# Splitting the search for each expert's first tokens over the end of one stage and the start of the next

## The reference

```python
xn = _layernorm(x, axis=-1)
s = _L0_attn_ref(xn, ...)      # two transformer blocks: norm, 2-head attention, norm, MLP of 512
g = _silu(_L0_ffn_ref(xn, ...))
x = x + s * g

# inside _L0_ffn_ref: 64 experts, each token goes to its 8 best, an expert keeps its first 64 tokens
probs = jax.nn.softmax(x @ router_w.T, axis=-1)
topk_w, topk_ids = jax.lax.top_k(probs, 8)
pos = jnp.cumsum(onehot, axis=0)[jnp.arange(N), flat_e] - 1
valid = pos < C                                   # C = 64
idx = jnp.where(valid, flat_e * C + pos, E * C)
x_buf = jnp.zeros((E * C + 1, x.shape[1]), x.dtype).at[idx].set(x[tok])
# per expert: silu(xb @ w_gate) * (xb @ w_up) @ w_down, weighted and added back to its tokens,
# plus a shared expert for all tokens
```

## Time and profile before

| | us |
|---|---|
| median of 3 runs | 1468.88 (1463.78 to 1471.66) |
| the profiled execution's own time | 1472.35 |
| its span in the trace | 1470.5 |
| TensorE matmuls busy | 1217.1 (83% of the span) |
| VectorE busy | 1017.4 (69%) |
| ScalarE busy | 784.7 (53%) |
| GpSimd busy | 655.8 (45%) |

### The profile page before, as it was taken

The page is one execution under the profiler, slowest core; times in us unless marked ns, Lnnn a source line. Parts: engine busy times, 40 slices in busy tenths (PEclk is TensorE's granted clock), DMA queues, the critical chain, the costliest instruction groups (busy, mean ns, idle before and its releaser), DMA issues. The chain is left out here.

```text
span 1470.5 us, 29231 instructions
## 1 busy us (share of the span) xinstructions
PE 1217.1 (83%) x7815; PEld 919.7 (63%) x7816; DVE 1017.4 (69%) x3639; ACT 784.7 (53%) x2010; POOL 655.8 (45%) x1270
## 2 busy tenths in 40 slices
PE   3999999999924999999999746568888888599993
PEld 2778777877722677777677534446666666366662
DVE  2777777777766777777777378757777777266663
ACT  1675656666512666566565356646666666233331
POOL 3343434434211545455454468714444444146665
PEclk9999999999966999999999855589999999699997
DMA  3433334242301221222212166534444444355562
GB/s 137 150 98 134 116 113 140 89 142 87 121 4 36 61 59 40 57 40 60 60 39 51 13 192 213 174 108 151 150 146 146 150 150 142 110 152 174 173 179 71
DMA packets 159257, 162.84 MB, mean 111 GB/s; under 512 B 20950, under 2 KB 138429, under 8 KB 159216
## 3 DMA queue, kind: packets, MB, share of 16 engines
q1 hardware_dynamic: 143936, 133.23, 29.0%
q0 software_dynamic: 14848, 26.77, 6.6%
q10 hardware_dynamic: 432, 2.38, 0.4%
HBM read 76.59 MB, written 71.04 MB: 100 GB/s over the span
## 5 line engine op out<-in xcount | busy, mean ns | idle before, releaser
L380 ACT ACTIVATE big<-ps,BHS 128x256 f32<-128x256 f32 x256 | 107.2, 470 | 61.1 <-PE ps L257 60.4
L257 PE MATMUL ps<-big,W 128*128 128x256 f32 x512 | 130.7, 400 | 5.9 <-ACT big L385 5.9
L392 ACT ACTIVATE pr<-ps,nmx 128x256 f32<-128x256 f32 x256 | 117.9, 473 | 27.4 <-DVE nmx L439 26.7
L270 PE MATMUL ps<-W,big 128*128 128x128 f32 x1024 | 130.9, 281 | 0.0
L270 PEld LDWEIGHTS ps<-W,big 128*128 128x128 f32 x1024 | 119.8, 192 | 13.9 <-ACT big L380 9.9
L2141 POOL DMA_INDIRECT out<-X,io x96 | 100.6, 1048 | 34.4 <-issue 34.4
L257 PEld LDWEIGHTS ps<-big,W 128*128 128x128 f32 x512 | 95.6, 197 | 27.3 <-ACT big L385 16.2
L1983 PE MATMUL ps<-big,zT 128*128 x192 | 103.3, 620 | 8.7 <-DVE pr L2079 8.4
L439 DVE TENSOR_REDUCE nmx<-ps 128x2 f32<-128x512 f32 x128 | 82.4, 686 | 40.4 <-PE ps L292 39.7
L1016 POOL DMA_INDIRECT ffn<-big,si x64 | 93.9, 1468 | 26.4 <-issue 26.4
L2057 ACT ACTIVATE pr<-ps 128x256 f32<-128x256 f32 x96 | 36.9, 384 | 108.2 <-PE ps L1983 108.2
(11 more groups left out here) (256 smaller groups left out, 3276.7 us busy)
## 6 DMA issues: line engine op xcount, KB each, us to landing
srt<-big SPq DMA_DIRECT2D x16, 1584.0 KB, 5.7
X<-srt SPq DMA_DIRECT2D x24, 800.0 KB, 4.6
big<-we SPq DMA_DIRECT2D x16, 768.0 KB, 4.9
rowd<-big SPq DMA_DIRECT2D x32, 272.0 KB, 2.2
big<-x SPq DMA_DIRECT2D x64, 128.0 KB, 2.2
X<-big SPq DMA_DIRECT2D x64, 128.0 KB, 2.1
big<-we SPq DMA_DIRECT2D x16, 384.0 KB, 3.5
X<-srt SPq DMA_DIRECT2D x24, 256.0 KB, 3.0
```

Source lines behind the costliest of these rows:

```text
L257: last = pe.matmul(pb[2 * g + f // 2][:, f % 2 * S:(f % 2 + 1) * S], W0[:, l, 512 + f * P:512 + (f + 1) * P], zT2[:, g, :], start=True, st ...
L270: last = pe.matmul(pb[4 + g][:, t * C:(t + 1) * C], hT[:, g, f, t * P:(t + 1) * P], W0[:, l, 1024 + f * C:1024 + (f + 1) * C], start=(f == ...
L380: act.activation(hT[:, g, f, :], pb[2 * g + half][:, f % 2 * S:(f % 2 + 1) * S], ACT.Silu, bias=BHS[:, l, f:f + 1], scale=GELU).then_inc(s ...
L392: last = act.activation(pr[:, g, h, t, :], pb[2 * g + h][:, t * S:(t + 1) * S], ACT.Exp, bias=nmx[:, g, h * TPU + t:h * TPU + t + 1], accu ...
```

## The change

The block `pick` is gone, with its two meetings of all engines reduced to the one between the stages. Its work is split:

- `bodies` takes a function `between`, called ahead of the last, feed-forward-only body. DVE in stage 1 passes one: it waits for all words (`keyT`, 16) and runs `pick_words`, the first search with its preparation and split (before: lines 909 to 906 of the first round). `result(0)` and `result(1)` come behind it.
- In stage 2 DVE does the statistics and the norm of pair 0 first and then `pick_tokens`: the second and third search, `firsts`, the wait for PE's turned list, and `gidx` and `sidx`. Only then comes the copy into `gi` that raises `idx`, and then the bodies.
- PE turns the list after its front for pair 0, then waits for a new semaphore `scaled`, and starts its bodies.
- POOL adds the unit matrix to W1 and scales W0 between its `front(0)` and its first `step`, and raises `scaled`.

The two functions and their helpers `largest` and `split` have the same instructions as before, on tiles of the same shapes.

```diff
-        def bodies(engine, step):
+        def bodies(engine, step, between=None):
             step(0, ffn=False)
             with engine.Fori(1, HALF - 1) as i:
                 step(i)
             step(HALF - 1, front=False)
+            if between:
+                between()
             step(HALF, att=False)
...
+        def pick_words(dve):
+            dve.scalar_tensor_tensor(work, words, 0.0, CST[0:E0, C_WORD:C_WORD + TOK // 16], ALU.is_gt, ALU.mult)
+            dve.drain()
+            dve.scalar_tensor_tensor(work, work, float(2 ** 24), words, ALU.subtract, ALU.add)
+            dve.drain()
+            largest(dve, work, -float(2 ** 25))
+            split(dve, 4, 3.0, 16, True)
+        def pick_tokens(dve):
+            largest(dve, work[:, 0:4 * CAP], 0.0)
+            split(dve, 1, 4.0, 1, False)
+            largest(dve, work[:, 0:4 * CAP], 0.0)
+            dve.tensor_copy(em[:, :], CST[0:CAP, C_ONE:C_ONE + E0]).then_inc(firsts, 1)
+            dve.wait_ge(turned_keys, 1)
...
+            dve.tensor_tensor(sidx[:, :], tk[:, :], em[:, :], ALU.add)
...
-                    bodies(dve, lambda i, att=True, ffn=True, front=True: body_vector(dve, s, i, 0, att, ffn, x))
+
+                    def between():
+                        dve.wait_ge(s["keyT"], HALF)
+                        pick_words(dve)
+                    bodies(dve, lambda i, att=True, ffn=True, front=True: body_vector(dve, s, i, 0, att, ffn, x), between)
         stage1()
...
-        pick()
...
                     front(0)
+                    for n in range(NP // C):
+                        pool.tensor_tensor(W1[:, n * C:(n + 1) * C], W1[:, n * C:(n + 1) * C], ident, ALU.add)
+                    pool.tensor_scalar(W0[:, 1, 1024:1536], W0[:, 1, 1024:1536], 1.0 / GELU, None, ALU.mult)\
+                        .then_inc(scaled, 1)
                     step(0, first=True)
...
                     x.front(pe, 0)
+                    pe.wait_ge(firsts, 1)
+                    for h in range(2):
+                        last = pe.matmul(pb[0][h * CAP:(h + 1) * CAP, 0:E0], lst[:, :], ident[0:E0, 0:E0],
+                                         start=True, stop=True)
+                    last.then_inc(turned_keys, 1)
+                    pe.wait_ge(scaled, 1)
                     bodies(pe, lambda i, att=True, ffn=True, front=True: body_tensor(pe, s, i, 1, att, ffn, x))
...
-                    dve.tensor_copy(gi[:, :], gidx[:, 0:EP]).then_inc(s["idx"], 1)
                     x.stats(dve, 0)
                     x.z1_of(dve, 0)
+                    pick_tokens(dve)
+                    dve.drain()
+                    dve.tensor_copy(gi[:, :], gidx[:, 0:EP]).then_inc(s["idx"], 1)
                     bodies(dve, lambda i, att=True, ffn=True, front=True: body_vector(dve, s, i, 1, att, ffn, x))
```

More of the change, by code:

```diff
@@ L558, in mixed_layers @@
         new_words = pb[6][0:E0, S:S + 2 * TPU * N_W]
+        lst = early([E0, CAP])
+        work = early([E0, TOK // 16])
+        part = early([E0, CAP, 4])
+        wide = early([E0, CAP])
+        li = early([E0, CAP]).bitcast(I32)
+        wi = early([E0, CAP]).bitcast(I32)
+        pi = early([E0, CAP, 4]).bitcast(I32)
+        kf = early([P, E0 // 2])
+        kf0 = early([CAP, E0])
+        tk = early([CAP, E0])
+        em = early([CAP, E0])
+        firsts, turned_keys = sem("p_firsts"), sem("p_turned")
@@ new lines, in mixed_layers, with largest, split @@
+        gidx = sb("gidx", [P, E0 // 2], I32)
+        sidx = sb("sidx", [CAP, E0], I32)
+        def largest(dve, src, least):
+            for r in range(CAP // 8):
+                dve.max(out=lst[:, 8 * r:8 * r + 8], in_=src)
+                dve.drain()
+                if r < CAP // 8 - 1:
+                    dve.match_replace(out=src, in_to_replace=lst[:, 8 * r:8 * r + 8], in_values=src,
+                                      imm_value=least)
+                    dve.drain()
+        def split(dve, bits, above, scale, signed):
+            dst = work[:, 0:4 * CAP].rearrange("p (w n) -> p w n", n=4)
+            dve.tensor_copy(li[:, :], lst[:, :])
+            dve.drain()
+            for n in range(4):
+                dve.tensor_scalar(pi[:, :, n], li[:, :], (3 - n) * bits, 2 ** bits - 1,
+                                  ALU.logical_shift_right, ALU.bitwise_and)
+            if signed:
+                dve.tensor_scalar(wi[:, :], li[:, :], 4 * bits, TOK // 16 - 1, ALU.logical_shift_right,
+                                  ALU.bitwise_and)
+                dve.drain()
+                dve.tensor_scalar(wi[:, :], wi[:, :], TOK // 32, 2, ALU.bitwise_xor, ALU.logical_shift_left)
+            else:
+                dve.tensor_scalar(wi[:, :], li[:, :], 4 * bits, 2, ALU.logical_shift_right,
+                                  ALU.logical_shift_left)
+            dve.drain()
+            dve.tensor_scalar(wide[:, :], wi[:, :], above, None, ALU.add)
+            dve.tensor_copy(part[:, :, :], pi[:, :, :])
+            dve.drain()
+            dve.tensor_tensor(dst, wide[:, :].unsqueeze(2).to_broadcast([E0, CAP, 4]),
+                              CST[0:E0, C_IOTA:C_IOTA + 4].unsqueeze(1).to_broadcast([E0, CAP, 4]), ALU.subtract)
+            dve.drain()
+            dve.scalar_tensor_tensor(dst, part[:, :, :], 0.0, dst, ALU.is_gt, ALU.mult)
+            dve.drain()
+            if scale > 1:
+                dve.scalar_tensor_tensor(dst, dst, float(scale), part[:, :, :], ALU.mult, ALU.add)
+                dve.drain()
@@ L830, in _ @@
                     x.stats(dve, 0)
-                    bodies(dve, lambda i, att=True, ffn=True, front=True: body_vector(dve, s, i, 0, att, ffn, x))
+                    def between():
+                        dve.wait_ge(s["keyT"], HALF)
+                        pick_words(dve)
+                    bodies(dve, lambda i, att=True, ffn=True, front=True: body_vector(dve, s, i, 0, att, ffn, x), between)
         stage1()
-        gidx = sb("gidx", [P, E0 // 2], I32)
-        sidx = sb("sidx", [CAP, E0], I32)
@@ L839, in pick @@
[L839 to L930, removed]
@@ L948, in stage2 @@
             s.update(sems("s2", ["xeTp", "xeT", "eg", "es", "eh", "ehTp", "ehT", "ey", "ye", "idx", "rstd1", "rstd2"]))
-            wg_in, wd_in = sem("s2_wg_in"), sem("s2_wd_in")
+            wg_in, wd_in, scaled = sem("s2_wg_in"), sem("s2_wd_in"), sem("s2_scaled")
             rows_in = [sem(f"s2_rows_in{j}") for j in range(EP)]
```

12 lines of the change are left out of this document (added).

## The result

The changed kernel takes 1456.51 us (median of 5 runs, 1451.84 to 1457.29) against 1468.88 us of the kernel before (5 runs, 1463.78 to 1472.14). The ratio is 0.9906, with a 95% interval from 0.9885 to 0.9926: faster by 0.9%, clear of the 0.5% that the prediction named. Its profiled execution took 1457.29 us, with a span of 1455.5.

A forecast was written before the change was run, and what follows sets the result against it. DVE's search alone was taken to set the time from 416.12 to 450.88 us. Line 430 of stage 2 moves from 464.88 to 451.85, saving 13.0 us: profiled 1472.35 to 1459.3, as a median 1456 us; range 1450 to 1464.6.

The forecast's parts named there:

- 1. First search: End of stage 1: 16.58 us of DVE's search start at 404.56, 11.2 us of it beside PE's work.
- 2. Additions and meeting: End of stage 1: two additions queue behind the search, 0.84 us, then 0.32 us for the meeting; stage 2 starts at 422.30.
- 3. Front: Start of stage 2: 6.80 us to the norm's end, plus 0.4 us (0 to 1.8) because POOL's additions meet the norm.
- 4. Second and third search: Stage 2 behind the norm: 18.18 us, 429.5 to 447.7, covering PE's, ACT's and POOL's work; PE's wait for `scaled` ends early.
- 5 and 7. The list and the clock: Stage 2, list to line 430: list turned at 448.2, line 430 at 451.2, plus 0.65 us for PE's half clock.
- 6. The gather: Body 0 of stage 2: rows there at 455.4, PE turns them at 455.8; costed at nothing, bound 1 us.
- (b): End of stage 1: first search not hidden, 11.2 us lost, 1467 us; chance 0.11 including other losses leaving under 7.3 us.
- (c): Body 0 and half of body 1, stage 2: PE's clock does not come back, net 9.5 us slower, 1478 us; chance 0.06.
- (d): Body 0 of stage 2: gather ends last because `idx` comes late, 1 us more, 1457 us; chance 0.73 together with the forecast.
- (a): All 34.8 us of DVE's search take 1.16 times as long beside other engines, 5.6 us more, 1461.5 us; chance 0.10.

The follow-up runs named there:

- words_part_only: Kernel before with only the first search moved beside stage 1's last feed-forward body, the other searches in their own block ahead of stage 2; 1458.73 us, ratio 0.9927.
- pool_early: Changed kernel with POOL's five additions and its scaling moved from stage 2 to the end of its work in stage 1; 1458.29 us, ratio 0.9912.
- pe_busy_longer: Changed kernel with 18 added matmuls, into a bank nobody reads, on PE between its front for pair 0 and its wait for the list; 1454.92 us, ratio 0.9882.
- words_after_body: Changed kernel with the first search called behind the last feed-forward body of stage 1 instead of ahead of it; 1467.11 us, ratio 0.9974.
- all_in_stage2: Changed kernel with the whole search behind the norm of pair 0 in stage 2, none beside stage 1; 1468.17 us, ratio 0.9992.
- after_again: The changed kernel once more, unchanged, on the same chip as pe_busy_longer; 1455.57 us, ratio 0.9894.

## Why the prediction was right

The forecast was 1456 us in a range from 1450 to 1465; measured are 1456.5. The saving up to line 430 was forecast as 13.0 us and is 13.4, or 13.2 without the earlier body 15. The mechanism is the one forecast. That the median came within 0.5 us is luck: five executions of the changed kernel lie 5.5 us apart, and the medians of before and after differ by 12.4 us.

1. First search: from its start to the additions 16.92 us against 16.58, the difference a wait of 0.34 us at line 582. It started at 404.29, 0.3 us ahead of the forecast. The cover came out as described: 10.2 us in words_part_only.
2. Additions and meeting: 1.04 us against 1.16.
3. Front: 7.27 us against 6.80 + 0.4. The norm took 0.60 us longer than before, where I had taken 0.4 between 0 and 1.8. The rule of the Trainium skill ("SBUF — State Buffer", "Who interferes with whom") that I had weighed is borne out in its direction by pool_early. The upper bound, 1.8 us, was three times too high: none of the four norm instructions waited for a whole addition, each was longer by about 0.15 us. The 1003 ns addition of the earlier trace rows was also not the only slow one: the five took 3.10 us together there and 2.10 us in pool_early.
4. Second and third search: 18.56 us against 18.18, with another such wait, 0.44 us at line 579. POOL's work ended at 431.5, and PE never waited for `scaled`.
5 and 7. The list and the clock: 3.43 us against 3.52 and an allowance of 0.65 for the clock. The allowance was not needed: at the new place PE was at half clock about as long. The clock comes back inside the microsecond from 453, with a mean of 0.67 in it:

```profile
453.00:454.00 1.00, 1.00 (x7) 0.88 (x8) 0.92 (x8) 0.00 (x0) 0.94 (x1) 0.67 0.35 98
```

This is some 5.1 us after line 277 against 4.7 before, and from line 430 to the maxima of line 439 are 3.56 us against 3.44. The allowance also stood in the wrong place. Line 430 follows line 277 by 2.97 us in both kernels, with PE at half clock all the way, so a clock that comes back later could only have cost something behind line 430, and the prediction added it ahead. The price of the half clock itself was measured in the changed kernel alone, 1.3 to 1.5 us by pe_busy_longer; that it is the same before, and so nearly nothing in the difference, is read from these equal stretches.
6. The gather: PE turned the rows at 456.28 without a wait for them, with about half a microsecond to spare (second issue at 453.06, landing 2.7 us later). The forecast had 0.4 us to spare, but by two errors that cancelled: from POOL's first instruction to the second issue were 2.56 us, not 2.01, and the landing took 2.7 us, not 3.1. The 0.2 us that it gave the semaphore stands in no row; here POOL starts 0.08 us after the copy ends. This was the thinnest margin, and in the two kernels with PE at full clock it is gone.

Errors cancelled in part. The way from the list to line 430 was priced 0.74 us too high, nearly all of it the allowance for the clock, and the search started 0.27 us early; against these stand 0.78 us of waits inside the search that no row of before had shown. Of the rivals, (b) is excluded by words_after_body and the start at 404.29, (c) by the clock's return, and (d) did not occur: PE had no wait for the gathered rows. For (a) the prediction had named a sign, searches longer than 16.6 and 18.2 us, and this sign did appear, with 16.92 and 18.56. But the excess is no more than the two waits of 0.34 and 0.44 us, and what company costs the first search, 0.10 us at line 619, it had cost at line 911 before. The sign was drawn too tight to tell these apart. One reading of the 40 slices was also loose: the search fills most of the slice with the 2, but only 9.8 of the 36.8 us of the slice with the 4 (441.1 to 450.9). The sum did not use it.

## What to carry to other kernels

A serial piece on one engine that stands between two phases is hidden in parts, each beside work that does not need that engine, and each part is worth what runs beside it: here 10.2 us came from the end of one phase and only about 3 us from the start of the next. After such a split read the waits of the serial engine again; the 3.1 and 1.5 us that it still waited were filled with pieces of the same search for about another 4 us. And where a change is smaller than the scatter of the untouched parts, compare markers in the trace ahead of and behind the change instead of spans.

## What was not expected of the hardware

- DVE waits 0.34 us and 0.44 us ahead of an instruction at lines 582 and 579 with nothing that ends the wait but its issue. The second stood in every kernel with the search in stage 2, words_after_body included, and both at the same places in each repeat; the same instructions in the old block had none. The traces have one more thing to say: in all eleven with such waits, a transfer of 8 KB on a DMA queue of the kind "instruction" starts 0.7 to 0.9 us after each of them ends. For the second of the changed kernel (it ends at 445.30) it starts at 445.99, and the DMA view from 445.5 to 446.5 us has it alone:

```profile
q14 instruction: 1, 0.01, 2.0%
```

  That points at the loading of DVE's own instructions, and so at the place of the code and not at its company. It is not shown: before and words_after_body have one such transfer each inside the first search (424.36 and 424.56 us) with no wait ahead of it, and no run moved the code alone.
- POOL and DVE hold each other up in both directions. POOL's norm at line 531 beside the two-input instructions of lines 617 and 619 took 1.61 us, against 0.88 us for its two instructions in words_after_body, where DVE does nothing then; here it cost nothing, because DVE's search, and not PE's feed-forward body, ended the stage. In the front it was DVE's norm that got longer (1.11 to 1.71 us), while POOL's five additions took 2.10 us, as long as in pool_early, where they ran beside MAX8.
- PE ended stage 1's last body at different times in kernels that are the same up to there, from 412.8 to 416.9 us. The granted clock says why. Before, it fell at 405.1 us and was back at 412.0; in all_in_stage2 it fell at 403.4 and was back at 413.6, and the same eight matmuls of line 257 took 3.78 us instead of 2.65. In after_again it was low only from 403.6 to 407.0, and PE was done at 412.9. So the cover of the first search is not the same in each execution either: PE's last body ends from 9.2 to 12.1 us after DVE's body 15, and 10.8 us after it in the trace before. With the first search beside it, a late PE is hidden.
